# Four stacked graph layers on 64 graphs: maxima subtracted and sums made on VectorE instead of in ScalarE's exponential

## The chip, the cores and the metric

The kernel runs on one core of a Trainium2 chip. The metric is the device time of the program in microseconds (us), lower is better; several executions are made and their median is taken.

## The reference, cut to what matters

The input x holds 64 graphs of 128 nodes with 128 features each; all share one adjacency matrix of 128 by 128. Four layers follow each other, each with a residual and a layer norm. Layer 0 is a spectral filter, layer 1 two graph convolutions and LSTMs over windows of 1 to 4 nodes. The change touches the last two:

```
# layer 2, graph attention (edges)
Wh = h @ W ; s1 = Wh @ a1 ; s2 = Wh @ a2
e = s1[:, :, None] + s2[:, None, :]
e = where(e >= 0, e, 0.2 * e) ; e = where(adj == 0, -inf, e)
h_prime = softmax(e, axis=-1) @ Wh

# layer 3, attention with 4 heads of 32 features
scores = q @ k.T / sqrt(32) + mask      # mask: 0 or -inf, from adj
out = softmax(scores, axis=-1) @ v
```

## The kernel before

The program has three parts in a row. The first two (`spectral_basis`, `spectral_vectors`) work on the adjacency matrix alone: 127 reflections, then a bisection and the eigenvectors, about 710 us together. The third, `layers` (L689), does all the work on x, and the change lies in it alone.

`layers` takes the 64 graphs in groups of G = 4. Four groups are in flight, each in a slot s with its own tiles and its own two PSUM banks `P[s][0]` and `P[s][1]`; 4 slots by 4 graphs make a trip, and 4 trips (TRIPS) make the whole. The work of a slot is a list of stages. Slot s runs one stage behind slot s-1 (SKEW = 1), and the order of all (stage, slot) entries is sorted by this diagonal and, within a diagonal, by slot. Every engine walks through that same fixed list in order (`run`, L805) and does its own part of each entry (`stage`, one function for each engine). Engines meet by semaphores only, which count entries. The last stages of a trip are interleaved with the first four of the next trip. An engine that waits in one entry keeps everything behind it in the list waiting, of the other slots too.

The stages around the change:

- `edges`: TensorE makes s1 (four matmuls of one column each, L983), Wh (L899) and, once VectorE has copied s1 (L1220), s2 broadcast over the rows (L987). ScalarE copies Wh (L1046) and adds s1 as a bias (L1105) into t1.
- `edge_softmax`: VectorE applies the leaky rule (L1223), adds the mask (L1224), takes the maximum of each graph (L1226) and negates it into `ntop` (L1227). ScalarE then takes the exponential of each of the 4 graphs (L1111), 128 columns at a time, with `ntop` as the bias and `accum_out` into `total`, so that the subtraction and the sum are part of the same instruction.
- `edges_turned`, `attend`: TensorE transposes the unnormalised weights and multiplies by Wh, VectorE takes the reciprocal of `total` (L1230) and, in `attend`, scales and adds the residual (L1235).
- `scores`, `softmax`, `probs_turned`, `mixed`, twice, once for each pair r of heads. In `scores` TensorE makes 8 blocks (2 heads by 4 graphs, L1017) in both banks once the former pair's result has been copied. VectorE scales and masks each bank (L1245, two instructions of 512 columns), takes the maxima (L1250, 1024 columns into 8) and negates them (L1252). In `softmax` ScalarE takes 8 exponentials of 128 columns (L1131) with bias and accumulator. In `probs_turned` TensorE transposes (L904), ScalarE copies the first half (L1046) and VectorE makes the reciprocal (L1256) and copies the second half (L1258). In `mixed` TensorE multiplies by v (L1031) and VectorE copies the result (L1263).
- `heads_turned`, `norm_3`, `apply_3`: the results are transposed back, scaled (L1267), added to x (L1272), normalised (L1170 to L1180) and written out. GpSimd does the power -1/2 of each norm (L880). `apply_` stages are ScalarE's (L1057).

Of the kernel before, what the change touches and what calls it, by code (L numbers as in the profile page):

```python
# [15 lines left out]
N = 128  # L16
# [539 lines left out]
G = 4  # L556
# [132 lines left out]
def layers(nc, sb, psum, sem, c, ident, U, UT, x_dram, out_dram):  # L689
# [5 lines left out]
    def tiles(name, shape):  # L695
        return [sb(f"{name}_{s}", shape) for s in range(SLOTS)]
# [22 lines left out]
    shift = tiles("shift", [N, G])  # L719
    s1 = tiles("s1", [N, G])  # L720
    top = tiles("top", [N, PAIR * G])
    ntop = tiles("ntop", [N, PAIR * G])
    total = tiles("total", [N, PAIR * G])
    share = tiles("share", [N, PAIR * G])
    head_share = tiles("head_share", [N, HEADS // PAIR, PAIR * G])
# [89 lines left out]
    def waiter(engine):  # L815

        def at(name, occurrences, k, s, trip):
            engine.wait_ge(S_(name), trip * (len(occurrences) * SLOTS) + rank(occurrences, k, s))  # L820

        def on(name, s, trip):
            engine.wait_ge(S_(name), trip * SLOTS + (s + 1))

        def on_step(name, p, t, s, trip):
            what = "cell" if name in ("cell_tanh_ready", "h_ready") else "gates"
            first = "output" if name in ("gates_fo_ready", "acts_o_ready") else what
            at(name, [(first, 1, 0)] + [(what, *step) for step in steps[1:]], steps.index((p, t)), s, trip)

        def on_later(name, p, t, s, trip):  # L830
            at(name, [("gates", *step) for step in later], later.index((p, t)), s, trip)

        def on_norm(name, layer, s, trip):
            if name == "sum_ready":
                at(name, ["back", "sequence_back", "attend", "heads_turned"], layer, s, trip)
            else:
                at(name, [f"norm_{n}" for n in range(total_norms)], layer, s, trip)

        def on_windows(p, s, trip):
            at("windows_ready", [("cell", n - 1, n - 2) for n in range(CONTIGUOUS_FROM, PERIODS + 1)], p - CONTIGUOUS_FROM,  # L840
               s, trip)

        def on_pair(name, r, s, trip):
            what = {"masked": "scores", "tops": "scores", "tops_ready": "scores", "scores_ready": "scores",
                    "probs_ready": "softmax", "mixed_ready": "mixed", "mixed_copied": "mixed"}.get(name, "probs_turned")
            at(name, [(what, n) for n in range(HEADS // PAIR)], r, s, trip)

        return on, on_step, on_later, on_norm, on_pair, on_windows

    with nc.Block() as block:  # L850
# [190 lines left out]
        def _(act):  # L1041
# [6 lines left out]
            def stage(s, trip, name):  # L1048
# [43 lines left out]
                elif name[0] == "cell":  # L1092
                    _, p, t = name
                    m = G * windows(p)
                    on_step("cell_ready", p, t, s, trip)
                    A_.activation(gg[s][:, 0:m], cell[s][:, 0:m], ACT.Tanh, scale=0.5).then_inc(S_("cell_tanh_ready"), 1)
                elif name == "turn_2":
                    on("x2_turned", s, trip)
                    copy(flat(xT, s), P[s][1][:], "x2T_copied", s)
                elif name == "edges":  # L1100
                    on("wh_ready", s, trip)
                    copy(flat(wh, s), P[s][1][:], "wh_copied", s)
                    on("s2_ready", s, trip)
                    for b in range(G):
                        last = A_.activation(t1[s][:, b * N:(b + 1) * N], P[s][0][:, b * N:(b + 1) * N], ACT.Identity,  # L1105
                                             bias=s1[s][:, b:b + 1])
                    last.then_inc(S_("edges_ready"), 1)
                elif name == "edge_softmax":
                    on("gat_top_ready", s, trip)
                    for b in range(G):  # L1110
                        last = A_.activation(t2[s][:, b * N:(b + 1) * N], t2[s][:, b * N:(b + 1) * N], ACT.Exp,  # L1111
                                             bias=ntop[s][:, b:b + 1], accum_out=total[s][:, b:b + 1])
                    last.then_inc(S_("attention_ready"), 1)
                elif name == "edges_turned":
                    on("attention_turned", s, trip)
                    copy(t3[s][:], P[s][1][:], "attentionT_copied", s)
                elif name == "turn_3":
                    on("x3_turned", s, trip)
                    copy(flat(xT, s), P[s][1][:], "x3T_copied", s)
                elif name == "qkv":  # L1120
                    on("q_ready", s, trip)
                    copy(flat(qT, s), P[s][0][:], "q_copied", s)
                elif name == "values":
                    on("v_ready", s, trip)
                    copy(flat(wh, s), P[s][0][:], "v_copied", s)
                elif name[0] == "softmax":
                    on_pair("tops_ready", name[1], s, trip)
                    for h in range(PAIR):
                        for b in range(G):
                            k = h * G + b  # L1130
                            last = A_.activation(S[s][:, h, b, :], S[s][:, h, b, :], ACT.Exp, bias=ntop[s][:, k:k + 1],  # L1131
                                                 accum_out=total[s][:, k:k + 1])
                    last.then_inc(S_("probs_ready"), 1)
                elif name[0] == "probs_turned":
                    on_pair("probs_turned_a", name[1], s, trip)
                    copy(ST[s][:, 0].rearrange("n g m -> n (g m)"), P[s][0][:], "probsT_copied_a", s)
# [4 lines left out]
        def _(v):  # L1141
# [10 lines left out]
            def stage(s, trip, name):  # L1152
# [68 lines left out]
                elif name == "edge_softmax":  # L1221
# [2 lines left out]
                    link(V.tensor_tensor(grouped(t2, s), grouped(t1, s), c["mask"][:, None, :].to_broadcast([N, G, N]),  # L1224
                                         ALU.add), "gat_masked")
                    link(V.reduce_max(top[s][:, 0:G], grouped(t2, s), AX_X), "gat_tops")  # L1226
                    signal(V.tensor_scalar(ntop[s][:, 0:G], top[s][:, 0:G], -1.0, None, ALU.mult), "gat_top_ready", s)  # L1227
                elif name == "edges_turned":
                    on("attention_ready", s, trip)
                    signal(V.reciprocal(share[s][:, 0:G], total[s][:, 0:G]), "gat_share", s)  # L1230
                elif name == "attend":
                    on("gat_ready", s, trip)
# [8 lines left out]
                elif name[0] == "scores":  # L1241
# [5 lines left out]
                                                      ALU.mult, ALU.add)  # L1247
                    signal(last, "masked", s)
                    on_pair("masked", r, s, trip)
                    signal(V.reduce_max(top[s][:], S[s][:].rearrange("n h g m -> n (h g) m"), AX_X), "tops", s)  # L1250
                    on_pair("tops", r, s, trip)
                    signal(V.tensor_scalar(ntop[s][:], top[s][:], -1.0, None, ALU.mult), "tops_ready", s)  # L1252
                elif name[0] == "probs_turned":
                    r = name[1]
                    on_pair("probs_ready", r, s, trip)
                    signal(V.reciprocal(head_share[s][:, r, :], total[s][:]), "head_share", s)  # L1256
                    on_pair("probs_turned_b", r, s, trip)
                    signal(V.tensor_copy(ST[s][:, 1].rearrange("n g m -> n (g m)"), P[s][1][:]), "probsT_copied_b", s)  # L1258
# [76 lines left out]
```

## Time and profile before

| | |
|---|---|
| median of 3 runs | 1529.11 us (1529.09 to 1530.44) |
| the profiled execution | 1530.87 us |
| its span | 1529.2 us |
| instructions in the span | 26912 |

The profile is that of one execution. Busy times are sums over the span; a share of the span is an average over the three parts of the program. The views used below are: the page's list of engines, sums over a stretch of time, instructions in order of time, who waited for whom, groups of instructions by line and shape, and the chain of work that ended last, which is followed back from the last instruction to what released each step. PE is TensorE, DVE is VectorE, ACT is ScalarE. Consecutive instructions of an engine overlap a little, so that the distance of their starts is below the duration of one.

### The profile page before, as it was taken

What the parts mean: (1) busy time and instruction counts of PE and PEld (TensorE: products, weight loads), DVE (VectorE), ACT (ScalarE), POOL (GpSimd) and SP (SyncE); (2) the same over time, 40 slices, a digit from 0 to 9 for tenths busy, and PEclk for the clock granted to TensorE, in tenths of its full rate; (3) what the DMA queues carried; (4) which work ended last, traced back from release to release, by engine and by line L of the source; (5) the groups of instructions that cost most, each with busy time, mean ns of one, the idle gap of its engine ahead of it and who ended that gap; (6) DMA issues with size and microseconds to landing.
All of it is one profiled execution on the core that took longest, in us unless ns stands there. A gap on an engine that the chain in (4) does not pass through costs nothing.

```text
span 1529.2 us, 26912 instructions
## 1 busy us (share of the span) xinstructions
PE 1087.6 (71%) x6198; PEld 888.0 (58%) x6198; DVE 1181.6 (77%) x5525; ACT 825.4 (54%) x2800; POOL 195.9 (13%) x441
## 2 busy tenths in 40 slices
PE   7888888888820000006998879988789979899884
PEld 5777777777610000004797666886668956679763
DVE  7999999999989898994455785566865667845677
ACT  4555555555510000003677776767867768667776
POOL 2122221122200000001011111111020120201111
PEclk9999999999995555557998999988999988999898
DMA  0000000000020000001000001000010000000000
GB/s 2 0 0 0 0 0 0 0 0 0 0 74 0 1 1 1 1 0 48 8 1 1 1 27 32 1 2 1 2 57 1 1 1 1 29 1 1 1 1 29
DMA packets 19857, 12.50 MB, mean 8 GB/s; under 512 B 1153, under 2 KB 18722, under 8 KB 19746
## 3 DMA queue, kind: packets, MB, share of 16 engines
q1 hardware_dynamic: 19746, 11.23, 2.6%
q8 instruction: 44, 0.72, 0.2%
q14 instruction: 67, 0.55, 0.1%
HBM read 7.03 MB, written 4.19 MB: 7 GB/s over the span
## 4 chain that ended last, share of the span: by engine, by line
PE 33%; DVE 10%; ACT 7%; issue 2%; POOL 1%; DMA 0%; DVEq 0%; POOLq 0%; ACTq 0%
PE P L954 10%; PE P L899 7%; PE P L962 5%; PE P L904 3%; ACT x L1057 2%; ACT S L1131 2%; PE P L987 1%; DVE S L1245 1%; DVE top L1250 1%; PE P L1017 1%; DVE stats L1170 1%; DVE t L1263 1%; PE P L971 1%; PE P L983 1%; PE P L1001 1%
## 5 line engine op out<-in xcount | busy, mean ns | idle before, releaser
L402 PE MATMUL sumP<-tail_ident,Yb 128*128 128x128 f32 x1 | 0.5, 477 | 215.5 <-DVE Yb L546 215.5
L179 PE MATMUL productP<-M,tail_ident 128*128 128x128 f32 x254 | 101.0, 501 | 57.5 <-DVE M L297 57.5
L411 ACT ACTIVATE small<-small 128x1 f32<-128x1 f32 x1 | 0.2, 203 | 236.3 <-DVE small L519 236.3
L954 PE MATMUL P<-t,WihT 128*128 128x128 f32 (+1 forms) x832 | 119.4, 290 | 9.7 <-POOL t L887 9.7
L402 PEld LDWEIGHTS sumP<-tail_ident,Yb 128*128 128x128 f32 x1 | 0.2, 183 | 215.6 <-DVE Yb L546 215.6
L880 POOL TENSOR_TENSOR rstd<-variance,minus_half 128x4 f32<-128x4 f32 x64 | 64.5, 1007 | 460.2 <-DVE variance L1180 460.2
L962 PE MATMUL P<-step_h,WhhT 128*128 128x128 f32 (+2 forms) x768 | 123.4, 304 | 0.0
L179 PEld LDWEIGHTS productP<-M,tail_ident 128*128 128x128 f32 x254 | 63.8, 312 | 95.0 <-DVE M L297 95.0
L954 PEld LDWEIGHTS P<-t,WihT 128*128 128x128 f32 x832 | 109.9, 191 | 13.2 <-POOL t L887 12.5
L1080 ACT ACTIVATE gate_i<-P,half_bias 128x128 f32<-128x128 f32 (+3 forms) x160 | 69.1, 432 | 88.1 <-PE P L962 65.3
L962 PEld LDWEIGHTS P<-step_h,WhhT 128*128 128x128 f32 x768 | 108.9, 191 | 4.5 <-DVE step_h L1213 0.7
L1200 DVE SCALAR_TENSOR_TENSOR gate_i<-gate_i,gate_g 128x128 f32<-128x128 f32 (+2 forms) x96 | 38.3, 399 | 84.5 <-ACT gate_g L1080 84.5
L176 PE MATMUL tailP<-tail_ident 128*128 128x129 f32 x254 | 101.5, 502 | 0.9 <-DVE tail_ident L247 0.9
L184 PE MATMUL p_rowP<-M,v_col 128*128 128x128 f32 x254 | 99.7, 496 | 0.8 <-DVE v_col L265 0.8
L157 POOL TENSOR_TENSOR QT<-QT,z_scaled 128x128 f32<-128x128 f32 x127 | 57.5, 453 | 329.0 <-ACT z_scaled L216 329.0
L1131 ACT ACTIVATE S<-S,ntop 128x128 f32<-128x128 f32 x256 | 98.6, 391 | 0.0
L954 PE MATMUL P<-HT,WihT 128*128 128x256 f32 (+1 forms) x288 | 84.8, 433 | 0.0
L1057 ACT ACTIVATE x<-x,shift,rstd 128x128 f32<-128x128 f32 x192 | 78.8, 486 | 4.1 <-POOL shift L882 3.9
L186 PE MATMUL zP<-QT,v_col 128*128 128x128 f32 x254 | 80.6, 421 | 0.0
L176 PEld LDWEIGHTS tailP<-tail_ident 128*128 128x128 f32 x254 | 63.7, 311 | 23.5 <-DVE tail_ident L283 22.3
L1080 ACT ACTIVATE gate_o<-P,half_bias 128x128 f32<-128x128 f32 (+3 forms) x160 | 70.3, 440 | 8.5 <-PE P L971 8.5
L1197 DVE SCALAR_TENSOR_TENSOR cell<-gate_i,gate_g 128x512 f32<-128x512 f32 (+3 forms) x64 | 27.9, 436 | 55.5 <-ACT gate_g L1080 54.9
(289 smaller groups left out, 3272.6 us busy)
## 6 DMA issues: line engine op xcount, KB each, us to landing
xin<-x SPq DMA_DIRECT2D x16, 256.0 KB, 2.9
out<-y SPq DMA_DIRECT2D x16, 256.0 KB, 2.3
W<-L_gnn_W SPq DMA_DIRECT2D x3, 64.0 KB
Wqkv<-L_gnn_W SPq DMA_DIRECT2D x1, 192.0 KB
Wg<-L_gnn_Wg SPq DMA_DIRECT2D x2, 64.0 KB
A<-adj SPq DMA_DIRECT2D x1, 64.0 KB, 1.9
b<-L_gnn_b SPq DMA_DIRECT2D x1, 64.0 KB
bg<-L_gnn_bg SPq DMA_DIRECT2D x1, 64.0 KB
```

Source lines behind the costliest of these rows:

```text
L157: nc.gpsimd.tensor_tensor(QT[:], QT[:], z_scaled[:], ALU.add).then_inc(q_ready, 1)
L176: pe.matmul(tailP[:, 0:1 + N], tails, tail_ident[:], start=True, stop=True).then_inc(tail_row_ready, 1)
L179: pe.matmul(productP[:, 0:N], tails, M[:], start=True, stop=True).then_inc(product_ready, 1)
L184: pe.matmul(p_rowP[:, 0:N], reflector, M[:], start=True, stop=True).then_inc(p_row_ready, 1)
L186: pe.matmul(zP[:, 0:N], reflector, QT[:], start=True, stop=True).then_inc(z_ready, 1)
L880: nc.gpsimd.tensor_tensor(rstd[s][:], variance[s][:], minus_half[:], ALU.pow).then_inc(S_("rstd_ready"), 1)
L899: last = pe.matmul(out[:, b * H:(b + 1) * H], lhs(b), rhs(b), start=True, stop=True)
L954: last = pe.matmul(place, c["WihT"][:, p - 1, gate * H:(gate + 1) * H], sources(s, p, t), start=bank not in fresh, stop=not t, skip_group_ ...
L962: last = pe.matmul(gate_place(s, p, t, gate), c["WhhT"][:, p - 1, gate * H:(gate + 1) * H], step_h[s][:, 0:G * windows(p)], start=False, s ...
L1057: last = A_.activation(to[s][:, b, :], x[s][:, b, :], ACT.Identity, bias=shift[s][:, b:b + 1], scale=rstd[s][:, b:b + 1])
L1080: return A_.activation(tile[s][:, 0:m], gate_place(s, p, t, gate), ACT.Tanh, bias=bias[:, k:k + 1], scale=scale)
L1131: last = A_.activation(S[s][:, h, b, :], S[s][:, h, b, :], ACT.Exp, bias=ntop[s][:, k:k + 1], accum_out=total[s][:, k:k + 1])
```

## The change

On VectorE the negation of the maxima is replaced by a subtraction of the maxima from all scores, in place, with the maxima broadcast over 128 columns: 512 columns for the edges and 1024 for a pair of heads. ScalarE's 4 or 8 exponentials of 128 columns become one of 512 or 1024 columns, without bias and without accumulator. VectorE makes the sums from the exponentials, ahead of the reciprocal that was there before. The semaphores `gat_top_ready` and `tops_ready` give way to `gat_shifted` and `shifted`, and `gat_totals` and `totals` are new: VectorE waits for its own sum before the reciprocal. The tile `ntop` goes.

```diff
--- before.py
+++ after.py
@@ -719,7 +719,6 @@
     shift = tiles("shift", [N, G])
     s1 = tiles("s1", [N, G])
     top = tiles("top", [N, PAIR * G])
-    ntop = tiles("ntop", [N, PAIR * G])
     total = tiles("total", [N, PAIR * G])
     share = tiles("share", [N, PAIR * G])
     head_share = tiles("head_share", [N, HEADS // PAIR, PAIR * G])
@@ -841,7 +840,7 @@
                s, trip)
 
         def on_pair(name, r, s, trip):
-            what = {"masked": "scores", "tops": "scores", "tops_ready": "scores", "scores_ready": "scores",
+            what = {"masked": "scores", "tops": "scores", "shifted": "scores", "scores_ready": "scores",
                     "probs_ready": "softmax", "mixed_ready": "mixed", "mixed_copied": "mixed"}.get(name, "probs_turned")
             at(name, [(what, n) for n in range(HEADS // PAIR)], r, s, trip)
 
@@ -1106,11 +1105,8 @@
                                              bias=s1[s][:, b:b + 1])
                     last.then_inc(S_("edges_ready"), 1)
                 elif name == "edge_softmax":
-                    on("gat_top_ready", s, trip)
-                    for b in range(G):
-                        last = A_.activation(t2[s][:, b * N:(b + 1) * N], t2[s][:, b * N:(b + 1) * N], ACT.Exp,
-                                             bias=ntop[s][:, b:b + 1], accum_out=total[s][:, b:b + 1])
-                    last.then_inc(S_("attention_ready"), 1)
+                    on("gat_shifted", s, trip)
+                    A_.activation(t2[s][:], t2[s][:], ACT.Exp).then_inc(S_("attention_ready"), 1)
                 elif name == "edges_turned":
                     on("attention_turned", s, trip)
                     copy(t3[s][:], P[s][1][:], "attentionT_copied", s)
@@ -1124,13 +1120,8 @@
                     on("v_ready", s, trip)
                     copy(flat(wh, s), P[s][0][:], "v_copied", s)
                 elif name[0] == "softmax":
-                    on_pair("tops_ready", name[1], s, trip)
-                    for h in range(PAIR):
-                        for b in range(G):
-                            k = h * G + b
-                            last = A_.activation(S[s][:, h, b, :], S[s][:, h, b, :], ACT.Exp, bias=ntop[s][:, k:k + 1],
-                                                 accum_out=total[s][:, k:k + 1])
-                    last.then_inc(S_("probs_ready"), 1)
+                    on_pair("shifted", name[1], s, trip)
+                    A_.activation(S[s][:], S[s][:], ACT.Exp).then_inc(S_("probs_ready"), 1)
                 elif name[0] == "probs_turned":
                     on_pair("probs_turned_a", name[1], s, trip)
                     copy(ST[s][:, 0].rearrange("n g m -> n (g m)"), P[s][0][:], "probsT_copied_a", s)
@@ -1224,9 +1215,11 @@
                     link(V.tensor_tensor(grouped(t2, s), grouped(t1, s), c["mask"][:, None, :].to_broadcast([N, G, N]),
                                          ALU.add), "gat_masked")
                     link(V.reduce_max(top[s][:, 0:G], grouped(t2, s), AX_X), "gat_tops")
-                    signal(V.tensor_scalar(ntop[s][:, 0:G], top[s][:, 0:G], -1.0, None, ALU.mult), "gat_top_ready", s)
+                    signal(V.tensor_tensor(grouped(t2, s), grouped(t2, s), top[s][:, 0:G, None].to_broadcast([N, G, N]),
+                                           ALU.subtract), "gat_shifted", s)
                 elif name == "edges_turned":
                     on("attention_ready", s, trip)
+                    link(V.reduce_sum(total[s][:, 0:G], grouped(t2, s), AX_X), "gat_totals")
                     signal(V.reciprocal(share[s][:, 0:G], total[s][:, 0:G]), "gat_share", s)
                 elif name == "attend":
                     on("gat_ready", s, trip)
@@ -1247,12 +1240,16 @@
                                                       ALU.mult, ALU.add)
                     signal(last, "masked", s)
                     on_pair("masked", r, s, trip)
-                    signal(V.reduce_max(top[s][:], S[s][:].rearrange("n h g m -> n (h g) m"), AX_X), "tops", s)
+                    every = S[s][:].rearrange("n h g m -> n (h g) m")
+                    signal(V.reduce_max(top[s][:], every, AX_X), "tops", s)
                     on_pair("tops", r, s, trip)
-                    signal(V.tensor_scalar(ntop[s][:], top[s][:], -1.0, None, ALU.mult), "tops_ready", s)
+                    signal(V.tensor_tensor(every, every, top[s][:, :, None].to_broadcast([N, PAIR * G, N]), ALU.subtract),
+                           "shifted", s)
                 elif name[0] == "probs_turned":
                     r = name[1]
                     on_pair("probs_ready", r, s, trip)
+                    signal(V.reduce_sum(total[s][:], S[s][:].rearrange("n h g m -> n (h g) m"), AX_X), "totals", s)
+                    on_pair("totals", r, s, trip)
                     signal(V.reciprocal(head_share[s][:, r, :], total[s][:]), "head_share", s)
                     on_pair("probs_turned_b", r, s, trip)
                     signal(V.tensor_copy(ST[s][:, 1].rearrange("n g m -> n (g m)"), P[s][1][:]), "probsT_copied_b", s)
```

## Rows read from the trace of the kernel before

**Rows 1.** The page's list of engines: busy us (share of the span) and instructions.

```profile
PE 1087.6 (71%) x6198; PEld 888.0 (58%) x6198; DVE 1181.6 (77%) x5525; ACT 825.4 (54%) x2800; POOL 195.9 (13%) x441
```

**Rows 2.** Sums over the heads' stretch: us; busy PE, PEld, DVE, ACT, POOL; clock; DMA.

```profile
1271.00:1315.00 44.00, 36.14 (x347) 28.43 (x347) 38.65 (x81) 34.96 (x149) 1.22 (x2) 0.87 0.00 1
```

**Rows 3.** VectorE in order of time: start us, us, line, operation [idle before].

```profile
1287.19 1.29 DVE L1245 SCALAR_TENSOR_TENSOR S<-P,mask 128x512 f32<-128x512 f32 x2
1288.52 1.22 DVE L1250 TENSOR_REDUCE top<-S 128x8 f32<-128x1024 f32 x1
1289.78 0.17 DVE L1252 TENSOR_SCALAR ntop<-top 128x8 f32<-128x8 f32 x1
1289.86 0.68 DVE L1263 COPY t<-P 64x512 f32<-64x512 f32 x1
1290.46 0.18 DVE L1256 RECIPROCAL head_share<-total 128x8 f32<-128x8 f32 x1
1290.57 0.63 DVE L1258 COPY ST<-P 128x512 f32<-128x512 f32 x1
1292.71 1.29 DVE L1245 SCALAR_TENSOR_TENSOR S<-P,mask 128x512 f32<-128x512 f32 x2 [1.52 <-PE P L1017]
```

**Rows 4.** Waits, all of the layers: us in total, times, longest.

```profile
DVE S L1245 <- PE P L1017: 15.0, 24, 1.5
```

**Rows 5.** Groups by line, ScalarE's exponentials of the heads: busy, mean ns, idle before.

```profile
L1131 ACT ACTIVATE S<-S,ntop 128x128 f32<-128x128 f32 x256 | 98.6, 391 | 0.0
L1131 ACT ACTIVATION_READ_ACCUMULATOR S<-S,ntop 128x1 f32 x256 | 48.9, 191 | 0.0
```

**Rows 6.** The chain that ended last, one pair's exponentials: start us, us, what.

```profile
1274.54 3.17 ACT S L1131 x16
```

**Rows 7.** Groups by line, ScalarE's tanh of the cell, two shapes.

```profile
L1096 ACT ACTIVATE gate_g<-cell 128x128 f32<-128x128 f32 x64 | 19.6, 322 | 0.9 <-DVE cell L1205 0.9
...
L1096 ACT ACTIVATE gate_g<-cell 128x512 f32<-128x512 f32 x16 | 10.3, 645 | 0.0
```

**Rows 8.** Groups by line, VectorE operations nearest to the new ones.

```profile
L449 DVE TENSOR_REDUCE count<-negative 128x16 f32<-128x2048 f32 x4 | 14.3, 3567 | 0.1
...
L1224 DVE TENSOR_TENSOR t<-t,mask 128x512 f32<-128x512 f32 x16 | 11.1, 692 | 0.6
...
L1226 DVE TENSOR_REDUCE top<-t 128x4 f32<-128x512 f32 x16 | 11.0, 686 | 0.5
...
L428 DVE TENSOR_TENSOR q<-D,shift 128x2048 f32<-128x2048 f32 x4 | 9.2, 2292 | 0.1
...
L448 DVE TENSOR_SCALAR negative<-q 128x2048 f32<-128x2048 f32 x4 | 4.9, 1226 | 0.1
```

**Rows 9.** TensorE in order of time, behind the heads' second scores.

```profile
1290.59 2.08 PE L1017 MATMUL P<-kT,qT 32*128 32x128 f32 x16 [2.79 <-DVE t L1263]
1292.59 1.92 PE L1031 MATMUL P<-ST,wh 128*32 128x128 f32 x16
...
1300.76 1.10 PE L904 MATMUL P<-tail_ident,S 128*128 128x128 f32 x8 [0.76 <-ACT S L1131]
1301.96 1.16 PE L1017 MATMUL P<-kT,qT 32*128 32x128 f32 x16
...
1303.73 1.07 PE L1031 MATMUL P<-ST,wh 128*32 128x128 f32 x16
```

**Rows 10.** Groups by line, VectorE's copy of turned probabilities.

```profile
L1258 DVE COPY ST<-P 128x512 f32<-128x512 f32 x32 | 21.8, 681 | 2.5 <-PE P L904 2.1
```

**Rows 11.** The chain that ended last, in the edges of one trip.

```profile
1251.04 0.17 DVE s L1220
...
1251.25 1.12 PE P L987 x2
...
1254.43 0.08 DVE share L1230
...
1257.08 1.34 ACT t L1111 x7
```

## The prediction, made before the changed kernel was run

> **What bounds the kernel now.** I read the page from the top and then went into the two places that the change touches. The busy shares come first: VectorE is the busiest engine at 77%, TensorE follows at 71%, and ScalarE has slack at 54% [rows 1]. That alone says which way work should not be moved, but it is an average over three programs in a row (the reflections, the bisection, the layers), so it has to be asked again where the softmaxes are. The heads' softmax of one trip runs within 44 us. There VectorE is busy for 38.65 us, 88%, ScalarE for 34.96 and TensorE for 36.14 [rows 2]. The four slots run one stage apart, and scores, softmax, probs_turned and mixed are four stages in a row, so in the middle of the stretch each diagonal holds one of each, for four different slots.
>
> The timeline of VectorE shows what such a diagonal is made of [rows 3]: two masked additions (1.29 us), the maximum over 1024 columns (1.22), its negation (0.17, and the next instruction begins 0.08 after it), the copy of the mixed heads (0.68), the reciprocal of the totals (0.18) and the copy of half the turned probabilities. From 1287.19 to the end of that copy at 1291.2 there is no hole, then comes one of 1.52 us in which VectorE waits for the next scores. All such holes together, over four trips, are 15.0 us in 24 waits [rows 4], 3.75 us a trip. So VectorE is nearly full in this stretch, and what is idle in it is small and countable.
>
> ScalarE spends 391 ns on each exponential of 128 columns and 191 ns on the read of its accumulator, 256 times each [rows 5]; consecutive ones overlap, so that a pair of heads (8 of them) takes 3.17 us from first to last in the chain that ended last [rows 6]. In this trip the chain goes through two such groups, the second a little shorter, and through a good deal of VectorE around them.
>
> **The change part by part.** *ScalarE, heads.* Sixteen instructions become one exponential over 1024 columns. The trace has none so long. The tanh without a pointer operand, SBUF to SBUF, takes 322 ns at 128 columns and 645 at 512 [rows 7], 0.84 ns a column; carried on, 1024 columns cost about 1.08 us. Bounds: 0.8 us if the price per column fell, 2.3 if it were two tanhs of 1024 columns. Against 3.17 us that is 2.1 us less per pair, 32 times, 67 us of ScalarE's work. The Trainium skill (ScalarE: Activation LUTs, What ACT_TABLE_LOAD costs) gives 186 ns plus 0.833 ns a column for an activation with immediates, an estimate of 1.04 us; by it ScalarE would save 1.3 us more over all pairs, off the path.
>
> *VectorE, heads.* The negation goes (0.17 us, 0.09 of VectorE's step) and a subtraction over 1024 columns comes. Its nearest rows are a subtraction with a broadcast over 2048 columns at 2292 ns and an addition with a broadcast mask over 512 columns at 692 ns, both with everything in SBUF [rows 8]. Between them 1.04 ns a column and 0.16 us fixed: 1.22 us, of which an independent successor sees some 1.14. Net +1.05 us. Then the sum over 1024 columns: the maximum of the same shape is the nearest row, 1.22 us [rows 3], and since the reciprocal waits for it, 1.26. Together +2.31 us per pair of heads and slot, 8 times a trip: +18.5 us. Bounds: if the subtraction had the price per column of the compare of 2048 columns, 1226 ns [rows 8], it would cost 0.7 us; if the sum had that of the strided sum of 2048 elements, 3567 ns [rows 8], it would cost 1.8 to 1.9. I take the middle rows because shape, strides and number of operands agree with them. Over 32 rounds the ends are -17 us and +20 us.
>
> *What of it is covered.* I take the instructions of VectorE in their order, push each back by what is new ahead of it, and let a hole swallow what it can. The first hole of a trip before scores, some 0.8 us, lies ahead of anything new and stays; the others of the 3.75 us [rows 4] swallow 2.9. The largest shows how: in the hole of 1.52 us [rows 3] 1.26 us of it go to the new sum, which stands between the copy of the mixed heads and the next scores; the rest stays, because TensorE starts those scores after that copy and needs 2.08 us for them [rows 9]. The copies of turned probabilities waited 2.5 us over the four trips [rows 10], 0.6 a trip, all swallowed, and two copies of keys some 0.3 a trip. That is about 4 us, and 14 to 14.5 of the 18.5 are left; I take 14. From there VectorE goes without a hole through heads_turned and norm_3 into the next trip's first stages, and TensorE's and ScalarE's waits hang on it, so nothing gives the 14 us back. What ScalarE saves falls into time in which it will wait for VectorE.
>
> *What is late next.* A diagonal in the middle asks of VectorE 1.32+1.26+1.14 for scores, 0.6 for mixed, 1.26+0.13+0.6 for the probabilities: 6.3 us. ScalarE needs 1.1 for the exponential and some 0.6 for its half of the turned probabilities, TensorE 1.16+1.07+1.10 at full clock [rows 9]. VectorE becomes the only bound.
>
> *Edges.* Four exponentials and four reads (about 1.6 us) become one of 512 columns (0.65). VectorE adds a subtraction of 512 columns for the negation (692 against the negation's 170 ns; in steps of VectorE +0.53) and a sum, for which the maximum of 512 columns stands, 686 ns [rows 8], in steps 0.73. The subtraction is queued ahead of the copy of s1 for the next slot, and TensorE's matmul of L987 waits for that copy; the sum is queued ahead of the next slot's leaky rule. The chain shows both places: s (L1220) and then L987, later share (L1230), behind which the leaky rule of the next slot stands [rows 11]. For the second slot the subtraction is hidden behind TensorE, for the third 0.43+0.73 us come, for the fourth 0.53+0.73, and at the end, where the chain goes from the negation through the exponentials of L1111 to ScalarE's apply_2 [rows 11], 0.45 is gained. Sum: +2.0 us a trip.
>
> *The rest.* The semaphores gat_shifted, shifted, gat_totals and totals take the places of gat_top_ready and tops_ready and add two waits on VectorE's own last result, counted above as 0.04 us each. No DMA and no GpSimd instruction changes. The bisection and the reflections are untouched.
>
> **Sum:** 4 trips of 14+2.0 us are +64 us. The profiled execution took 1530.87 us (span 1529.2), 1.8 us above the median of the runs; it would become 1595, and the median of 1529.1 becomes 1593 us. A measurement of this kernel tells some 0.2%, 3 us, from no change.
>
> **The rivals.**
> *The exponentials are what the rounds wait for (faster).* For it: two groups of exponentials stand on the chain of this trip, one of them 3.17 us [rows 6]. If VectorE's additions stayed within its idle time, each would shorten by 2.1 us and the end of the edges by 0.45: 4.65 us a trip, 18 us, 1511 us. It decides for this one if the 18.5 us find cover. Against it: the holes before scores are 3.75 us a trip [rows 4]. A page's rule would lead there: the Trainium skill (ScalarE: Activation LUTs, Rules for kernel authors) wants additions and maxima on VectorE rather than ScalarE. The subtraction was free in ScalarE's bias here, and VectorE is the fuller engine [rows 1, 2], so I give this 4%.
>
> *The extra work is nearly covered (same or a little slower).* If the holes in the stages behind the heads took up the delay as well, because x for the next trip has long been loaded, some 0 to 30 us would be left, 1529 to 1559. Against it: VectorE feeds TensorE in order there. 6%.
>
> *TensorE's clock falls too (slower still).* The scores that began after 2.79 us of idle time took 2.08 us where they otherwise take 1.16 [rows 9]; the granted clock of the whole stretch is 0.87 [rows 2], so part of it ran at 1.2 GHz and part at 2.4. The new diagonals leave TensorE idle about half the time. At the low level a diagonal is 2.08+1.92 and about 1.97 for the transposes (1.10 scaled as the scores are), 6.0 us, still just under VectorE's 6.3; but then each set of scores would arrive late behind its copy by some 0.1 to 0.3 us, and the stages right behind the heads would begin slow, about half a dozen groups of matmuls by 0.8 us each, of which VectorE's backlog covers part. I put that at 2 to 4 us a trip: 1601 to 1609. 15%.
>
> *The program does not do what it says.* If the compiler split the long exponential, ScalarE would still be below VectorE; this gives the forecast.
>
> **How the numbers follow.** Forecast 75%: 1593, its own range 1576 to 1613 by the bounds of the two new operations. The range of 8 in 10 reaches from 1570 to 1612; left out are the gain and most of the cover case on one side, and the joint worst of price and clock on the other. The chances of the sign: faster 0.05, the gain and a sliver of the cover case; within 0.2% 0.03 and the rest of the cover case slower; slower 0.92 in all.
>
> **What would show it.** In the profile of the changed kernel the subtraction should be near 1.22 us and the sum near 1.22, 32 times each; the exponential near 1.08; VectorE's busy time up by about 32 x 2.27 + 16 x 1.2 = 92 us to 1274, and over 95% in the middle of the heads, ScalarE's idle time there ending at the subtraction; the heads' stretch longer by 14 us; the waits for L1017 before the scores nearly gone. I would be wrong if holes remained on VectorE in that stretch, if the exponential took over 2 us, or if the stages behind the heads were shorter than now.

## The result and the profile after

The changed kernel takes 1599.85 us (median of 4 runs, 1598.73 to 1601.33) against 1529.78 (4 runs, 1529.09 to 1532.45): the ratio is 1.047, with a 95% interval of 1.0451 to 1.0488. It is 70 us slower. The prediction said 1593 with a range of 1570 to 1612, 64 us slower than its base; it was right in direction, in mechanism and, within a tenth, in size.

The page's span and list of engines, to be read against [rows 1]:

```profile
span 1597.3 us, 26368 instructions
PE 1118.2 (70%) x6198; PEld 913.6 (57%) x6198; DVE 1269.2 (79%) x5573; ACT 748.6 (47%) x2208; POOL 195.9 (12%) x441
```

ScalarE's busy time fell by 77 us and VectorE's rose by 88, and the span rose by 68. The time followed VectorE and took nothing from ScalarE. The same sums over 44 us of the heads of the same trip, from the first additions of scores (columns as in [rows 2]):

```profile
1308.00:1352.00 44.00, 31.11 (x296) 25.02 (x294) 42.92 (x56) 15.22 (x22) 0.00 (x0) 0.86 0.00 1
```

```profile
1307.75:1362.00 54.25, 38.33 (x332) 30.72 (x333) 52.81 (x78) 17.70 (x26) 1.22 (x2) 0.79 0.00 1
```

VectorE is now busy for 42.92 of 44 us, 97.5%, where [rows 2] had 38.65. ScalarE does less than half of what it did there. TensorE's granted clock is 0.86 in these 44 us and was 0.87 in those of [rows 2], but 0.79 over the whole of the longer stretch, the second row. Over the heads of all four trips it fell from 0.92, 0.96, 0.89 and 0.96 to 0.78 or 0.79. The trip of [rows 2] is the longest of the four before, 42.0 us where the others have 40.9.

The new operations, by line and shape (as [rows 5] and [rows 8]: busy us, mean ns, idle before):

```profile
L1124 ACT ACTIVATE S<-S 128x1024 f32<-128x1024 f32 x32 | 33.8, 1056 | 24.3 <-DVE S L1246 24.3
...
L1246 DVE TENSOR_TENSOR S<-S,top 128x1024 f32<-128x1024 f32 x32 | 39.2, 1225 | 1.1
...
L1251 DVE TENSOR_REDUCE total<-S 128x8 f32<-128x1024 f32 x32 | 38.7, 1210 | 0.4
...
L1222 DVE TENSOR_REDUCE total<-t 128x4 f32<-128x512 f32 x16 | 10.9, 678 | 2.5 <-ACT t L1109 2.5
```

Every price was met: the exponential 1.06 us (1.08 was said), the subtraction 1.225 (1.22), the sum 1.210 (1.22). VectorE in order of time, the diagonal that answers to [rows 3]:

```profile
1328.25 1.28 DVE L1238 SCALAR_TENSOR_TENSOR S<-P,mask 128x512 f32<-128x512 f32 x2
1329.57 1.22 DVE L1244 TENSOR_REDUCE top<-S 128x8 f32<-128x1024 f32 x1
1330.82 1.23 DVE L1246 TENSOR_TENSOR S<-S,top 128x1024 f32<-128x1024 f32 x1
1331.96 0.68 DVE L1260 COPY t<-P 64x512 f32<-64x512 f32 x1
1332.56 1.20 DVE L1251 TENSOR_REDUCE total<-S 128x8 f32<-128x1024 f32 x1
1333.80 0.20 DVE L1253 RECIPROCAL head_share<-total 128x8 f32<-128x8 f32 x1
1333.92 0.64 DVE L1255 COPY ST<-P 128x512 f32<-128x512 f32 x1
1334.82 1.29 DVE L1238 SCALAR_TENSOR_TENSOR S<-P,mask 128x512 f32<-128x512 f32 x2 [0.26 <-PE P L1016]
```

From one pair of additions to the next are 6.57 us where [rows 3] had 5.52. The hole of 1.52 us behind it has become one of 0.26, exactly what the walk left over (1.52 less 1.26 for the sum). Over the layers, what ScalarE waits for now, and last the wait that answers to [rows 4]:

```profile
ACT ST L1045 <- PE P L903: 110.8, 32, 6.3
...
ACT S L1124 <- DVE S L1246: 24.3, 16, 2.7
...
DVE S L1238 <- PE P L1016: 4.4, 8, 0.8
```

The 15.0 us in 24 waits of [rows 4] are down to 4.4 in 8: in each trip the first hole, up to 0.85 us, which lies ahead of anything new, and the 0.26 above. ScalarE's saving of 77 us reappears as waiting: its copy of the turned probabilities waited 23 us before and 110.8 now.

To see where the 68 us of the span lie, each trip can be cut at two points of VectorE's timeline: from the first leaky rule to the first addition of scores (called "edges" below, it ends with q, k and v of the first slot), and from there to the last reciprocal of the heads. Means over the four trips, worked out from the starts in the timelines, with the median times of all kernels of this study:

| kernel | edges, us | heads, us | median, us | ratio to before (95%) |
|---|---|---|---|---|
| before | 33.7 | 41.2 | 1529.8 | |
| the whole change | 36.9 | 55.4 | 1599.9 | 1.047 (1.0451 to 1.0488) |
| e1, edges only | 37.3 | 41.4 | 1546.2 | 1.0113 (1.0091 to 1.0134) |
| e2, heads only | 33.6 | 55.4 | 1584.7 | 1.0365 (1.0342 to 1.0388) |
| e3, heads, subtraction only | 33.3 | 47.2 | 1553.3 | 1.0166 (1.0143 to 1.0190) |
| e4, heads, sum only | 33.5 | 47.8 | 1557.6 | 1.0183 (1.0155 to 1.0212) |
| e5, short exponential only | 33.2 | 40.9 | 1530.9 | 1.0018 (1.0003 to 1.0034) |
| e6, sum twice | 37.0 | 64.0 | 1635.2 | 1.0701 (1.0678 to 1.0723) |
| e7, edges' sum late | 34.7 | 55.4 | 1589.4 | 1.0409 (1.0388 to 1.0430) |
| e8, one maximum, sum on VectorE | 33.7 | 47.8 | 1554.6 | 1.0172 (1.0149 to 1.0195) |
| e9, e7 and s1 copied early | 33.4 | 55.4 | 1585.0 | 1.0360 (1.0345 to 1.0375) |
| e10, e9's edges, old heads | 33.0 | 41.2 | 1527.9 | 0.9995 (0.9983 to 1.0007) |
| e11, copies on ScalarE | 37.3 | 45.7 | 1556.0 | 1.0168 (1.0153 to 1.0182) |
| e12, e8 with copies on ScalarE | 33.5 | 38.7 | 1514.4 | 0.9901 (0.9887 to 0.9915) |

Each ratio is to the runs of before on the same chip, so the medians of different rows are only good to a few us against each other. For the change: 4 times 14.2 us in the heads and 4 times 3.2 in the edges are 69.8, and the rest of the program is 1.6 us shorter.

### The profile page after: what moved, and what is told of

Same layout as the page of the kernel before. It is cut to its first block, busy times and chain, and to the rows that moved or that the text cites. A ratio compares the mean times of both kernels' runs of the same rounds, so it can differ in the third digit from the quotient of the medians.

```text
span 1597.3 us, 26368 instructions
## 1 busy us (share of the span) xinstructions
PE 1118.2 (70%) x6198; PEld 913.6 (57%) x6198; DVE 1269.2 (79%) x5573; ACT 748.6 (47%) x2208; POOL 195.9 (12%) x441
## 4 chain that ended last, share of the span: by engine, by line
PE 28%; DVE 19%; ACT 4%; issue 3%; POOL 1%; DMA 0%; DVEq 0%; POOLq 0%; ACTq 0%
PE P L953 10%; PE P L898 6%; PE P L961 5%; DVE S L1238 2%; DVE top L1244 2%; DVE total L1251 2%; DVE S L1246 2%; PE P L986 2%; ACT x L1056 2%; DVE stats L1161 1%; DVE t L1260 1%; DVE ST L1255 1%; PE P L903 1%; PE P L970 1%; PE P L1016 1%
## 5 line engine op out<-in xcount | busy, mean ns | idle before, releaser
L953 PEld LDWEIGHTS P<-t,WihT 128*128 128x128 f32 x832 | 109.9, 191 | 13.3 <-POOL t L886 12.5
L1045 ACT ACTIVATE ST<-P 128x512 f32<-128x512 f32 x32 | 19.1, 597 | 110.8 <-PE P L903 110.8
```

The source lines that it names most:

```text
L953: last = pe.matmul(place, c["WihT"][:, p - 1, gate * H:(gate + 1) * H], sources(s, p, t), start=bank not in fresh, stop=not t, skip_group_ ...
```

## The experiments

**e1 and e2, one part alone.** In e1 the heads are those of before, in e2 the edges are; every line is one of the two kernels', the loops over h and b left out:

```diff
 # e1: the heads as before
-A_.activation(S[s][:], S[s][:], ACT.Exp).then_inc(S_("probs_ready"), 1)
+last = A_.activation(S[s][:, h, b, :], S[s][:, h, b, :], ACT.Exp, bias=ntop[s][:, k:k + 1],
+                     accum_out=total[s][:, k:k + 1])
-signal(V.tensor_tensor(every, every, top[s][:, :, None].to_broadcast([N, PAIR * G, N]), ALU.subtract), "shifted", s)
+signal(V.tensor_scalar(ntop[s][:], top[s][:], -1.0, None, ALU.mult), "tops_ready", s)
-signal(V.reduce_sum(total[s][:], S[s][:].rearrange("n h g m -> n (h g) m"), AX_X), "totals", s)
 # e2: the edges as before
-A_.activation(t2[s][:], t2[s][:], ACT.Exp).then_inc(S_("attention_ready"), 1)
+last = A_.activation(t2[s][:, b * N:(b + 1) * N], t2[s][:, b * N:(b + 1) * N], ACT.Exp,
+                     bias=ntop[s][:, b:b + 1], accum_out=total[s][:, b:b + 1])
-link(V.reduce_sum(total[s][:, 0:G], grouped(t2, s), AX_X), "gat_totals")
```

Expected of e1:

> Only the edges are changed (one exponential of 512 columns, subtraction and sum on VectorE), the heads are as before. Theory, VectorE's order: the edges of a trip grew by 3.5 us between the two profiles (from the first leaky rule to the first additions of scores, 34.1 against 37.6), so 4 trips give +14 us, about 1544. Prediction's own sum for the edges: +2.0 a trip, +8 us, 1538. Rival, the edges grew only because TensorE came out of the longer heads at its slow clock: then this kernel, with the heads as before, is at +8 us or less.

Measured: +17 us (1.13% of 1529.3), 1546.2. Its edges take 37.3 us a trip, with the heads at 41.4 as before. The rival falls: the edges grow by themselves, and need no long heads before them.

Expected of e2:

> Only the heads are changed, the edges are as before. Theory: the heads' stretch grew by 13.3 us a trip in the profiles, so +53 us, about 1583; edges alone and heads alone add up to the whole change within 3 us. Rival, the two parts lean on each other through TensorE's clock: the two alone sum to clearly less than the +70 of the whole.

Measured: +55 us, 1584.7, the heads' stretch 55.4 us as in the whole change. 17 and 55 give 72 against the 70 of the whole; the parts add up. The 13.3 us of the expectation were read from the trip of [rows 2]; the mean over the four is 14.2.

**e3 and e4, one operation alone.** Both leave the edges as before.

```diff
 # e3: subtraction on VectorE, 8 exponentials with accumulator, no bias
-A_.activation(S[s][:], S[s][:], ACT.Exp)
+A_.activation(S[s][:, h, b, :], S[s][:, h, b, :], ACT.Exp, accum_out=total[s][:, k:k + 1])
-signal(V.reduce_sum(total[s][:], S[s][:].rearrange("n h g m -> n (h g) m"), AX_X), "totals", s)
 # e4: sum on VectorE, 8 exponentials with bias, no accumulator
-A_.activation(S[s][:], S[s][:], ACT.Exp)
+A_.activation(S[s][:, h, b, :], S[s][:, h, b, :], ACT.Exp, bias=ntop[s][:, k:k + 1])
-signal(V.tensor_tensor(every, every, top[s][:, :, None].to_broadcast([N, PAIR * G, N]), ALU.subtract), "shifted", s)
+signal(V.tensor_scalar(ntop[s][:], top[s][:], -1.0, None, ALU.mult), "tops_ready", s)
```

> In the heads alone the subtraction is on VectorE; ScalarE still makes 8 exponentials of 128 columns with the accumulator, but without bias; no sum on VectorE. Edges as before. Theory, VectorE is the bound: 8 times 1.05 us a trip less the holes it fills (some 2.5 us) give +6 a trip, +24 us, 1554 (bounds 16 to 34). Rival, the time of a round is the chain through the exponentials: nothing is covered and nothing gained, +34 us, 1564, and the exponentials stay on the chain that ended last.

Measured: 1553.3, +24 us; the heads take 6.0 us a trip more. By the distances of starts the 8 subtractions take 9.14 us of VectorE and the 8 negations that go had taken 0.93, so 8.2 came and 2.2 fell into idle time.

> In the heads alone the sum is on VectorE; ScalarE makes 8 exponentials with bias and without accumulator, the maxima are negated as before. Edges as before. Theory: 8 times 1.26 us a trip less the holes (the one of 1.5 us behind the copy of the mixed heads above all, some 3.5 us) give +6.6 a trip, +26 us, 1556 (bounds 18 to 40). Rival, the sum lies beside TensorE's transposes and costs nothing: 1529, or less by what ScalarE's missing reads of the accumulator give.

Measured: 1557.6, +28 us; 6.6 us a trip more in the heads: the sums take 9.95, and 3.3 fell into idle time. The sum does not lie beside the transposes for free. The two give 52 us together, and both at once with the short exponential 55 (e2). That it is more and not less fits idle time that can be filled once only (2.2 and 3.3 us apart, 3.9 together). The merging of 8 exponentials into one, which e2 has over e3 and e4, shows no gain there; no run has both operations with eight exponentials, and the direct tests of the merging are e5, and e8 against e4.

**e5, the short exponential alone.** This kernel leaves out the subtraction of the maxima and the sum; its outputs are scaled by other numbers.

```diff
 on_pair("tops_ready", name[1], s, trip)
-last = A_.activation(S[s][:, h, b, :], S[s][:, h, b, :], ACT.Exp, bias=ntop[s][:, k:k + 1],
-                     accum_out=total[s][:, k:k + 1])
+A_.activation(S[s][:], S[s][:], ACT.Exp).then_inc(S_("probs_ready"), 1)
 # the loops over h and b left out
-V.reciprocal(head_share[s][:, r, :], total[s][:])
+V.reciprocal(head_share[s][:, r, :], ntop[s][:])
```

> The kernel before, but in the heads ScalarE makes one exponential of 1024 columns without bias and accumulator. Left out: nothing is subtracted from the scores and no sum is made; VectorE still makes the maxima and their negation and takes the reciprocal of those, so its work is that of before. It shows what ScalarE's saving is worth alone. Theory, VectorE bounds the heads: the holes left in it are 4 us a trip and only part of them hang on the exponentials, so -1 to -3 us a trip, 1517 to 1526. Rival, the exponentials are what the rounds wait for: two groups on the chain of each trip, 2.1 us each and what follows from them, -17 us or more, up to 8 times 2.1 a trip, 67 us; below 1512.

Measured: 1530.9 against 1528.6, a ratio of 1.0018, at best no change: even the 1 to 3 us a trip that I expected did not come. The heads' stretch is 40.9 against 41.2 us. Rows of its trace say why: the exponential takes 2.1 us less per pair, ScalarE's copy of the turned probabilities waits for 71.7 us where it had waited for 23, and VectorE's wait for the scores is unchanged from [rows 4].

```profile
L1128 ACT ACTIVATE S<-S 128x1024 f32<-128x1024 f32 x32 | 33.7, 1053 | 8.2 <-DVE ntop L1247 7.5
```

```profile
ACT ST L1046 <- PE P L904: 71.7, 32, 4.6
...
DVE S L1240 <- PE P L1017: 15.1, 24, 1.5
```

The holes of VectorE do not hang on the exponentials. They stand behind its own copies, through TensorE: copy of the mixed heads, scores, additions. TensorE too only waited for something else: before, its transposes waited for the exponentials for 8.2 us in all and its scores for that copy for 11.1; in e5 the first are gone and the second are 17.8. A place on the chain that ended last [rows 6] did not mean that the time would shrink with it: with the exponentials shorter by 2 us the rounds still took as long. This is the run that decides against the first rival.

**e6, the sum twice.**

```diff
+V.reduce_sum(spare[s][:], S[s][:].rearrange("n h g m -> n (h g) m"), AX_X)
 signal(V.reduce_sum(total[s][:], S[s][:].rearrange("n h g m -> n (h g) m"), AX_X), "totals", s)
```

> The changed kernel with the sum of the heads made twice, the first into a spare tile. Theory: VectorE has no holes left in the heads, so all of it lands on the time: 32 times 1.13 to 1.22 us, +36 to +39, 1636 to 1639. Rival, part of VectorE's work is still covered: below +30.

Measured: 1635.2, +35 us on the changed kernel. The stretch of the heads grew by 8.67 us. By the distances of starts the 8 additional sums take 9.04 us, 1.13 each; 0.26 of it is the one hole that the changed kernel had left, which is gone in e6, and 0.1 comes off the copies behind. So in the changed kernel what VectorE gets more in the heads goes to the time nearly in full; the 1.13 that I had put as the lower end was the price, and that 35 us lie just under 36 is the hole.

**e7 and e9, the same work in another place.** Both are the changed kernel with VectorE's instructions of the edges reordered.

```diff
 # e7: the edges' sum and reciprocal in attend
 elif name == "edges_turned":
-    on("attention_ready", s, trip)
-    link(V.reduce_sum(total[s][:, 0:G], grouped(t2, s), AX_X), "gat_totals")
-    signal(V.reciprocal(share[s][:, 0:G], total[s][:, 0:G]), "gat_share", s)
+    pass
 elif name == "attend":
+    on("attention_ready", s, trip)
+    link(V.reduce_sum(total[s][:, 0:G], grouped(t2, s), AX_X), "gat_totals")
+    signal(V.reciprocal(share[s][:, 0:G], total[s][:, 0:G]), "gat_share", s)
     on("gat_ready", s, trip)
 # e9: in addition the copy of s1 stays in edges for s = 0 alone; for the others it is
 # in edge_softmax of the slot before, between the maximum and the subtraction
+    if s + 1 < SLOTS:
+        on("s1_ready", s + 1, trip)
+        signal(V.tensor_copy(s1[s + 1][:], P[s + 1][0][:, 0:G]), "s1_copied", s + 1)
```

> The changed kernel, but the sum and the reciprocal of the edges are made in the stage attend, ahead of the wait for TensorE's product, and not in edges_turned. There VectorE stood idle for 2 us before L1228 in the changed profile, and the sum is no longer ahead of the next slot's leaky rule. Theory, VectorE's order makes the edges longer: 0.73 us for each of two slots a trip comes back, -6 us, 1594. Rival, TensorE's clock or ScalarE is what makes the edges longer: within 2 us of 1600.

Measured: 1589.4, -10 us, where -6 was expected. The edges' stretch fell from 36.9 to 34.7 us.

> As the run with the edges' sum made late, and in addition VectorE copies s1 of the next slot ahead of the edges' subtraction instead of behind it, so that TensorE's matmul of L987 no longer waits for the subtraction. Same work on every engine. Theory, the edges grew by what is queued behind the two new instructions and by TensorE at 1.2 GHz after it had waited for s1: another 0.5 to 1 us for each of up to 3 slots a trip comes back, -6 us against the 1589 of that run, 1583; the edges' stretch then about 33.7 us as before the change. Rival, the place of the copy is of no account: 1588 to 1591.

Measured: 1585.0, another -4 us, the edges' stretch at 33.4, under the 33.7 of before. What the edges had cost came from the two places in the queue and from what those did to TensorE. The last step of the four slots shows the latter. TensorE and VectorE of the changed kernel, in order of time, to be read against [rows 11]:

```profile
1287.44 0.15 DVE L1211 COPY s<-P 128x4 f32<-128x4 f32 x1
...
1287.65 1.52 PE L986 MATMUL P<-xT,wa 128*128 128x512 f32 x2 [2.41 <-DVE s L1211]
...
1288.96 1.92 PE L898 MATMUL P<-wh,t 128*128 128x128 f32 x8
...
1290.92 1.12 DVE L1228 SCALAR_TENSOR_TENSOR x<-P,share,x 128x128 f32<-128x128 f32 x4 [1.80 <-PE P L898]
```

The sums over the stretch of these two groups of matmuls, first of the changed kernel, then of the same place in the kernel before:

```profile
1287.65:1290.85 3.20, 3.20 (x11) 2.45 (x12) 1.40 (x11) 2.16 (x6) 1.21 (x2) 0.59 0.00 0
```

```profile
1251.25:1253.25 2.00, 2.00 (x12) 1.52 (x13) 1.40 (x11) 2.00 (x10) 0.45 (x1) 1.00 0.00 0
```

The granted clock is 0.59 against 1.00: TensorE had stood idle for 2.41 us, waiting for the copy of s1, and ran mostly at 1.2 GHz afterwards; the same two groups took 3.2 us and not 2.0. The wait is 2.41 us in each of the four trips, with the clock at 0.58 to 0.61 behind it. In e7 it is 1.62 us; behind it the clock is 0.54 to 0.57 in three trips and 1.00 in the first, so the length of the wait alone does not say what comes. In e9 the wait is 0.59 us and the same groups are back at the times of before, 1.13 and 1.05 us:

```profile
1277.04 1.13 PE L986 MATMUL P<-xT,wa 128*128 128x512 f32 x2 [0.59 <-DVE s L1221]
1278.00 1.05 PE L898 MATMUL P<-wh,t 128*128 128x128 f32 x8
```

**e10, those edges on the old heads.** The diff is e9's on e1.

> The heads as in the kernel before, the edges changed as in the whole change, but with the sum made in attend and the copy of s1 ahead of the subtraction. Theory: the edges' part, +17 us when made alone, falls to nothing, 1526 to 1532, because in the edges VectorE has idle time and only the order hurt. Rival, the added work itself is on the path: 1535 or more.

Measured: 1527.9 against 1530.2, ratio 0.9995 (0.9983 to 1.0007), no difference. The work that e1 paid 17 us for is free in another order.

**e8, e11 and e12, towards a version that is faster.** In e8 a row has one maximum over all 8 blocks of a pair: a softmax allows any shift that is constant along its row, as long as the blocks of a row do not lie so far apart that the smaller ones vanish. ScalarE can then make one long exponential with that maximum as the bias, and VectorE need not subtract. In e11 and e12 ScalarE, which has time now, takes over two copies.

```diff
 # e8, on the kernel before; the negation is of one column, the eight exponentials go
-V.reduce_max(top[s][:], S[s][:].rearrange("n h g m -> n (h g) m"), AX_X)
+V.reduce_max(top[s][:, 0:1], S[s][:].rearrange("n h g m -> n (h g m)"), AX_X)
+A_.activation(S[s][:], S[s][:], ACT.Exp, bias=ntop[s][:, 0:1])
 # and the changed kernel's sum and wait for "totals" in probs_turned
 # e11 on the changed kernel, e12 on e8: ScalarE gets these, VectorE loses its own
+on_pair("probs_turned_b", name[1], s, trip)
+copy(ST[s][:, 1].rearrange("n g m -> n (g m)"), P[s][1][:], "probsT_copied_b", s)
+elif name[0] == "mixed":
+    on_pair("mixed_ready", name[1], s, trip)
+    copy(t2[s][pair, :], P[s][0][pair, :], "mixed_copied", s)
```

> The kernel before, but in the heads each row takes one maximum over all 8 blocks of a pair (a softmax allows any shift that is constant along its row), so ScalarE makes one exponential of 1024 columns with that maximum as bias, nothing is subtracted on VectorE, and the sum is on VectorE. Edges as before. Theory: the sum alone is on the path, less the holes, +5 to +7 us a trip, 1549 to 1558, as in the run with the sum alone; that ScalarE is 2 us shorter per pair makes hardly a difference between the two. Rival, the exponentials matter: clearly below the run with the sum alone.

Measured: 1554.6, ratio 1.0172; the run with the sum alone (e4) has 1.0183. The heads' stretch is 47.8 us in both. ScalarE spends 1144 ns per pair here against eight exponentials in e4, and it makes no difference.

> The changed kernel, but in the heads ScalarE also makes VectorE's two copies of a round (second half of the turned probabilities, mixed heads). Theory, VectorE is the bound and ScalarE has become idle: VectorE's diagonal falls by 1.2 us of 6.3, 8 times a trip, -38 us against the changed kernel, 1561, and still above the kernel before, because 5.1 us of VectorE are more than the 4.5 of before. Rival, the latency through the engines binds: gain below 15 us.

Measured: 1556.0, 44 us below the changed kernel and still 1.0168 of before. The stretch of the heads fell by 9.6 us a trip, 8 times 1.2, which are 39 of the 44 us; no run takes the other 5 apart.

> The kernel with one maximum per row and the sum on VectorE (1554.6), with the same two copies on ScalarE. VectorE's diagonal is then 1.32+1.26+0.09+1.26+0.13, 4.1 us, below the 4.5 of before; ScalarE's about 2.7, TensorE's 3.3 at full clock. Theory, VectorE's work alone sets the heads: -30 to -38 us, 1516 to 1525, faster than the kernel before. Rival, with VectorE so far down the waits for TensorE and the latencies between engines bind: 1530 to 1540.

Measured: 1514.4 us (4 runs, 1513.3 to 1515.3) against 1530.2, ratio 0.9901 (0.9887 to 0.9915): 1% faster than the kernel before and 5% faster than the changed one. The page's list of engines, and the sums over the stretch of the heads:

```profile
PE 1076.5 (71%) x6198; PEld 881.3 (58%) x6198; DVE 1175.8 (78%) x5493; ACT 798.0 (53%) x2384; POOL 195.5 (13%) x441
```

```profile
1261.00:1300.00 39.00, 32.77 (x362) 26.29 (x360) 36.86 (x66) 26.95 (x44) 1.22 (x2) 1.00 0.00 1
```

VectorE has 36.86 us in 39 of the heads, 94.5%: by this share it is the bound here too, with less to do. TensorE's granted clock is 1.00 in this stretch, and its share 84%; how much of the gain needs that clock, no run shows. The gain on e8 is 40 us, 36 of them in the heads (4 times 9.1), slightly more than the far end of what I had expected.

## Why the prediction was right, point by point

**The bound.** That VectorE is full in the heads and that holes are small and countable was right, and was the whole argument. e6 shows that the changed kernel has next to none left (0.26 us a trip), e5 that the old ones did not hang on ScalarE.

**The prices.** Subtraction 1.225 us and sum 1.210 us against 1.22 each; the exponential 1.056 against 1.08. The bounds on either side of them were not needed; the upper one of the exponential, said to be two tanhs of 1024 columns, is 2.2 us by the 1.08 beside it and not 2.3. The Trainium skill's formula for an activation with immediates (ScalarE: Activation LUTs, What ACT_TABLE_LOAD costs) gives an estimate of 1.04 us for it; the trace is 0.02 above.

**The walk through the holes.** 14 us a trip were said, 14.2 came. Its two terms hold as well: 18.5 us of work less about 4 of holes were said, and by the distances of starts the new operations less the negations are 18.2 us, of which 3.9 went into time that had been idle. The parts of the 4 were 2.9, 0.6 and 0.3, which leave 14.7; 14 was picked from "14 to 14.5", so that it came within 0.2 is in part luck. Each operation alone was swallowed in part as said, 2.2 of 8.2 us in e3 and 3.3 of 9.95 in e4.

**The edges.** This is the term that was mis-sized: +2.0 us a trip was said, +3.2 came (e1 alone: +3.6). The places were right, as e7 and e9 show by moving them; the step that failed is "for the fourth 0.53+0.73". The step from the third to the fourth slot's leaky rule took 8.15 us on average against 5.6, so 2.5 and not 1.26. The other 1.2 is TensorE at its lower clock, a term that the sum for the edges did not have: in the trip shown it had waited 2.41 us for the copy of s1, and two groups of matmuls took 3.2 us where they had taken 2.0. Smaller misses nearly cancel: the second slot's step was said to be hidden and cost 0.7, the third's 1.16 were 0.9, and the end gained 0.85 rather than 0.45; no run takes these apart. Four times 1.2, and four times 0.2 in the heads, are 5.6 of the 6 us between 64 and 70.

**The rivals.** The exponentials as the bound fell with e5. The extra work covered by the stages behind the heads did not happen: everything outside the two stretches is 1.6 us shorter and no more. TensorE's clock was given 15% as a case of the heads and what follows them. In the heads it fell (0.78 to 0.79 over the stretch, 0.89 to 0.96 before) and cost next to nothing: VectorE had one pause above 0.15 us there, the 0.26, and in e6, at 0.73, it had none; it cost in the edges, where I had not looked for it, and that moved the time most of the way to that rival's 1601. The measured time lies between the two.

**The busy time of VectorE** was said to reach 1274 us and reached 1269: I had added durations, of which overlapping neighbours count less.

## What to carry to other kernels

Ask where an operation goes, not how many instructions vanish. A bias and an accumulator in ScalarE's instruction cost time on an engine that had slack, the subtraction and the sum on their own cost it on the engine that had none; 77 us off ScalarE's busy time were worth nothing, 88 on VectorE's cost 70. Where an engine is nearly full in a stretch, walk its instructions in order and let each hole swallow what it can: that gave 14 of 14.2 us. Where it is not full, the place in its queue decides: the same two operations cost 17 us ahead of what others waited for, and nothing behind it. An engine freed by such a change should take work of the full one, as in e12.

## What the runs showed of the hardware that I had not expected

- A pointer as the bias has a price of its own. The exponential of 128 columns takes 391 ns with a bias tile [rows 5] and 295 in e3 without one, 1024 columns take 1144 ns in e8 and 1056 without; some 90 ns an instruction. The groups of e3 and e8:

```profile
L1131 ACT ACTIVATE S<-S 128x128 f32<-128x128 f32 x256 | 75.2, 295 | 16.7 <-DVE S L1253 16.7
```

```profile
L1128 ACT ACTIVATE S<-S,ntop 128x1024 f32<-128x1024 f32 x32 | 36.6, 1144 | 8.7 <-DVE ntop L1247 8.5
```

  The Trainium skill (ScalarE: Activation LUTs, What ACT_TABLE_LOAD costs) states 93 ns for each pointer operand; the traces agree.
- In the edges an idle time of TensorE of 2.41 us was followed by matmuls at mostly 1.2 GHz, so that a wait of two microseconds cost 1.2 more after it had ended. A wait of 1.62 us in e7 was followed by the same in three trips of four. In the heads of the changed kernel, at a granted clock of 0.79, and of e6, at 0.73, no such cost came through: the longest pause of VectorE in that stretch is 0.26 us in the one, and below 0.15 in the other.
